# First normalisation of a fused transformer block: from VectorE to ScalarE, with the shift computed on GpSimd

## The chip, the cores and the metric

One core of one Trainium2 chip. The time is device microseconds (us) of one execution. The engines are TensorE (PE in the profile; PEld is its weight load), VectorE (DVE), ScalarE (ACT), GpSimd (POOL) and SyncE (SP, whose queue issues DMAs). The chip's clock for TensorE has two levels, 1.2 and 2.4 GHz; the profile shows the granted share.

## The reference

The input x is 4 x 512 x 512 float32, that is 2048 rows of 512. Four residual blocks follow each other:

```
x = x + fp8_xattn(layernorm(x), ctx)          # stage a
x = x + gated_ffn(layernorm(x), gate, up, down)   # stage b, ternary weights, inner width 1408
x = x + cross_attention(layernorm(x), ctx, mask)  # stage c
x = x + hadamard_quantised_ffn(layernorm(x), ...) # stage d, inner width 2048
```

In stage a the normalised row is cut into blocks of 128, each block is scaled by 448 over its largest absolute value (at least 1e-4), rounded to float8 e4m3, scaled back, and multiplied with the context, which is quantised in blocks of 128 x 128 in the same way. The layernorm is (x - mean) / sqrt(var + 1e-5) per row.

## The kernel before, in words

X holds all rows in on-chip memory as 16 tiles of 128 rows x 512 (line 44). The engines run separate instruction lists, each written out by hand and joined by semaphores; an engine works through its own list strictly in order, so that a wait holds everything behind it. Stages a and b run together in 8 groups (`b_group(g)`, g = 0 to 7), about 33 to 36 us each. Group g does the feed-forward of tiles 2g and 2g+1 (stage b) and, beside it, stage a of tiles n0 = 2g+2 and n1 = 2g+3. Stages c and d follow. Tiles 0 to 2 of stage a are normalised ahead of the groups (lines 1187 to 1207).

Stage b of a group has 11 chunks c. For each, TensorE makes gate and up products (`gate_up_b`, L1725, 16 matmuls, about 1.75 us) in one of two PSUM banks, ScalarE takes Silu of the gate half (`b_silu`, L667), VectorE multiplies it with the up half (`b_hidden`, L1236), ScalarE writes the high half as float16 (`b_high`, L674), GpSimd the remainder (`h_low`, L494), and after all chunks TensorE multiplies down (`b_down`, L1740; the result is scaled and added on VectorE, L1250 and L1252). Chunk n of `gate_up_b` waits until `b_hidden` of chunk n-2 has emptied the bank:

```
wait(pe, b_h_r, n - 1)
```

Stage a of a tile j is spread between these: VectorE takes the row statistics (`a_stats`, L1042 to L1045), GpSimd the root of the variance (`root`, L464), VectorE normalises (`a_normal`, L1050) and takes the block maxima and scales (`a_smalls_of`, L1110, L1114, L1116), ScalarE applies the scales (`a_scale`, L617, L621), VectorE rounds to e4m3 (`a_grids` L1122 and L1124, `a_rounding` L1129 and L1135), SyncE's queue transposes by DMA (`a_turn`, L346), TensorE multiplies (`a_product`, L1677), and VectorE adds the four parts to X (`a_parts`, L1149). Tile n1 is done in the first half of the group, tile n0+2 (which is the next group's n0) is prepared at the end of it.

Around the changed places the lists read:

- GpSimd: `h_low(g, 0)`, `root` of a for n1, `h_low(g, 1)` and on; at the end of the group `root` of b and `b_center` (L470) for n1, `h_low(g, 10)`, `root` of a for n0+2.
- ScalarE: `b_silu` 1 and 2, `b_high` 0, (in group 1 `context_back(1, 3)` L608 and `context_high(1, 3)` L649), `b_silu` 3, in groups 1 to 6 `weight_sums` (L654, three long activations), `b_silu` 4, `b_high` 1 to 3, `a_scale(n1)`. At the end: `b_high` 10, `b_normal(n1)` (L641 and L645, stage b's normalisation with the shift of `b_center` as its bias), in odd groups `context_scaled` (L600), `a_scale(n0 + 2)`, in even groups `context_back` and `context_high`.
- VectorE: `b_hidden` 1, `a_stats(n1)`, `b_hidden` 2, context work, `a_normal(n1)`, context work, `b_hidden` 3 and 4, `a_smalls_of(n1)`, `a_parts(n0, 0)`, `a_grids(n1)`, `b_hidden` 5. At the end: `a_stats(n0 + 2)`, `a_normal(n0 + 2)`, `a_smalls_of(n0 + 2)`, `b_low(n1)` (L1170), in even groups `context_rounding(e, 3)` (L1088, L1090), `b_down(2g)`, `context_low(e, 2)` (L1174); the next group begins with `context_grid` in even groups, `a_grids(n0)`, `b_down` and `b_hidden` 0.

Of the kernel before, what the change touches and what calls it, by code (L numbers as in the profile page):

```python
# [7 lines left out]
P = 128  # L8
# [19 lines left out]
def fused_blocks(nc, x, ctx_t, ctx_n, mask, gate_t, up_t, down_t, gate_s, up_s, down_s,  # L28
# [7 lines left out]
    with ExitStack() as ctx:  # L36
# [16 lines left out]
        shift = sb("shift", [P, 2, 1])  # L53
        room = {"a": "a", "b": "b", "c": "a"}
# [158 lines left out]
        eps_tuple = sem("eps_tuple_ready")  # L213
        c_xh_r, c_xl_r, c_ph_r, c_pl_r, c_cv_hi, c_cv_first, c_cv_lo = (
# [245 lines left out]
        def _(pool):  # L460
            def root(g, j, u):
                r = room[g]
                pool.wait_ge(st_step[g], 3 * j + 3)
                nc.gpsimd.tensor_tensor(rstd[r][:, u, :], mv[r][:, u, 1:2], mhalf[:, :], ALU.pow).then_inc(st_rstd[g], 1)  # L464

# [30 lines left out]
            def b_group(g):  # L496
                more, n0, n1 = g + 1 < PAIRS, 2 * g + 2, 2 * g + 3
                h_low(g, 0)
                if more:
                    root("a", n1, 1)  # L500
                h_low(g, 1)
                h_low(g, 2)
                h_low(g, 3)
                h_low(g, 4)
                h_low(g, 5)
                if more:
                    root("b", n0, 0)
                    b_center(n0, 0)
                h_low(g, 6)
                h_low(g, 7)  # L510
                h_low(g, 8)
                h_low(g, 9)
                if more:
                    root("b", n1, 1)
                    b_center(n1, 1)
                h_low(g, 10)
                if n0 + 2 < NT:
                    root("a", n0 + 2, 0)

# [73 lines left out]
        def _(act):  # L593
# [28 lines left out]

            def a_back(j):
# [56 lines left out]
            def b_group(g):  # L680
# [17 lines left out]
                b_high(g, 0)  # L698
                if g == 1:
                    context_back(1, 3)  # L700
                    context_high(1, 3)
# [60 lines left out]
                if more:  # L762
                    b_normal(n1)
                if odd and following < B:
# [268 lines left out]
        def _(dve):  # L1033
            V = nc.vector

            def stats(g, j, u):
# [3 lines left out]
                if g == "b":  # L1040
                    wait(dve, b_shift, j - 3)
                V.bn_stats(bn[r][:, u, 0:6], tile_of(X, j)).then_inc(s, 1)  # L1042
# [211 lines left out]
            def b_group(g):  # L1254
# [40 lines left out]
                if more:  # L1295
                    a_normal(n1)
# [63 lines left out]
                if n0 + 2 < NT:  # L1360
                    a_normal(n0 + 2)
                    a_smalls_of(n0 + 2)
# [5 lines left out]
                if not odd and e < B and g:  # L1368
                    context_rounding(e, 3)
                if more:  # L1370
# [665 lines left out]
```

## Time and profile before

| | |
|---|---|
| median of 3 runs | 710.25 us (709.42 to 713.08) |
| the profiled execution | 712.37 us, its span 710.5 us |
| busy in the span: PE, DVE, ACT, POOL | 651.9, 573.7, 474.4, 368.0 us |
| groups 1 to 6 of stages a and b | 79.88 to 287.25 us of the span |
| granted clock in these groups | 1.00 of 2.4 GHz |

The busy share is a mean over stages. What a change in the groups is worth has to be read from the chain of waits inside a group: TensorE's list is the longest, and a stall in it is time lost for good. The profile numbers instructions by line of the kernel; where it says `x8` after a row of the timeline, eight like instructions were merged into it.

### The profile page before, as it was taken

The numbers are of one execution on the slowest core, as the hardware profiler recorded it, in microseconds if no ns is written. First come the engines' busy times: TensorE is split into PE (matmuls) and PEld (weight loads), VectorE is DVE, ScalarE is ACT, GpSimd is POOL, SyncE is SP. The second block draws the span as 40 slices with busy tenths as digits, with TensorE's granted clock in tenths as the row PEclk, the third lists the DMA queues.
The fourth block names the chain that finished last, engine by engine and source line by source line (L and its number), as shares of the span: only waits on it lengthen the run. The fifth ranks groups of instructions, "written<-read, shape, count | busy, mean of one in ns | idle before, by whom it ended". The sixth has DMA issues, their size and how long they took to land.

```text
span 710.5 us, 12399 instructions
## 1 busy us (share of the span) xinstructions
PE 651.9 (92%) x4086; PEld 375.4 (53%) x4086; DVE 573.7 (81%) x1255; ACT 474.4 (67%) x981; POOL 368.0 (52%) x291
## 2 busy tenths in 40 slices
PE   1689899999999999998898999897999999999996
PEld 0365566656666676753343444453545555555553
DVE  6889898989898887367687864777888888888874
ACT  3747567856776656378687842576778888778734
POOL 2023122323232413167566730069899999999970
PEclk9999999999999999999999999999999999999998
DMA  9971243434441422718999950344657655656611
GB/s 219 252 259 23 83 102 77 105 90 108 73 111 24 112 67 73 247 30 196 301 285 263 233 98 18 75 86 64 118 120 113 136 108 113 139 118 123 114 47 45
DMA packets 173130, 88.21 MB, mean 124 GB/s; under 512 B 150546, under 2 KB 152594, under 8 KB 172052
## 3 DMA queue, kind: packets, MB, share of 16 engines
q1 hardware_dynamic: 167188, 71.94, 45.5%
q10 hardware_dynamic: 3408, 11.27, 4.8%
q0 software_dynamic: 2480, 4.33, 3.4%
q8 instruction: 28, 0.46, 0.3%
q14 instruction: 26, 0.21, 0.1%
HBM read 51.20 MB, written 4.19 MB: 78 GB/s over the span
## 4 chain that ended last, share of the span: by engine, by line
PE 36%; DVE 28%; ACT 12%; issue 11%; POOL 7%; DMA 4%; SPq 1%; DVEq 0%; POOLq 0%; ACTq 0%
PE ps L1725 10%; PE ps L1820 6%; PE ps L1802 6%; PE ps L1740 4%; DVE y_sm L1549 4%; DMA arena<-arena 3%; PE ps L1878 3%; POOL arena L568 2%; POOL arena L569 2%; DVE ps L1509 2%; DVE arena L1236 2%; PE ps L1950 2%; ACT arena L936 2%; DVE X L1149 2%; ACT arena L919 2%
## 5 line engine op out<-in xcount | busy, mean ns | idle before, releaser
L1725 PE MATMUL ps<-arena 128*128 128x256 f16 x1408 | 161.1, 273 | 6.7 <-DVE arena L1236 4.9
L1725 PEld LDWEIGHTS ps<-arena 128*128 128x128 f16 x1408 | 135.2, 98 | 33.9 <-DVE arena L1236 10.3
L494 POOL TENSOR_TENSOR arena<-arena 128x256 f16<-128x256 f32 x88 | 58.9, 687 | 176.4 <-ACT arena L674 176.3
L1878 PE MATMUL ps<-arena 128*128 128x512 bf16 x512 | 118.9, 380 | 5.6 <-ACT arena L888 3.8
L568 POOL TENSOR_TENSOR arena<-arena 128x1024 f32<-128x1024 f32 x44 | 103.7, 2358 | 31.9 <-DVE arena L1523 28.6
L569 POOL TENSOR_TENSOR arena<-arena 128x1024 f32<-128x1024 f32 x44 | 104.0, 2364 | 0.0
L1740 PE MATMUL ps<-arena 128*128 128x512 f16 x352 | 80.0, 385 | 5.7 <-POOL arena L494 5.7
L1878 PEld LDWEIGHTS ps<-arena 128*128 128x128 bf16 x512 | 48.0, 98 | 65.2 <-DVE arena L1515 7.5
L667 ACT ACTIVATE arena<-ps,gs 128x256 f32<-128x256 f32 x88 | 40.8, 467 | 55.1 <-PE ps L1725 55.1
L1820 PE MATMUL ps<-arena 128*128 128x512 f16 x256 | 59.4, 387 | 6.0 <-DMA arena<-arena 3.5
L1950 PE MATMUL ps<-arena 128*128 128x512 bf16 x256 | 61.4, 386 | 1.9 <-ACT arena L966 1.9
L1740 PEld LDWEIGHTS ps<-arena 128*128 128x128 f16 x352 | 34.2, 99 | 48.5 <-POOL arena L494 9.0
L1509 DVE SCALAR_TENSOR_TENSOR ps<-ps,f_sm,arena 128x512 f32<-128x512 f32 x60 | 45.1, 753 | 17.1 <-ACT arena L910 17.1
L910 ACT ACTIVATE arena<-ps,f_sm 128x512 f32<-128x512 f32 x64 | 44.2, 692 | 17.9 <-PE ps L1878 16.8
L1236 DVE SCALAR_TENSOR_TENSOR arena<-ps,us,arena 128x256 f32<-128x256 f32 x88 | 41.5, 476 | 17.5 <-ACT arena L667 16.6
L1802 PE MATMUL ps<-arena 128*128 128x512 f16 x240 | 53.9, 379 | 1.1 <-DMA arena<-arena 1.1
L936 ACT ACTIVATE arena<-ps 128x512 f16<-128x512 f32 x60 | 35.6, 594 | 26.4 <-DVE ps L1509 26.4
L1515 DVE TENSOR_TENSOR arena<-ps,arena 128x512 f16<-128x512 f32 x60 | 41.3, 688 | 12.7 <-ACT arena L936 12.4
L919 ACT ACTIVATE arena<-arena,y_sm 128x1024 f32<-128x1024 f32 x32 | 36.3, 1144 | 17.7 <-DVE y_sm L1561 17.7
L1820 PEld LDWEIGHTS ps<-arena 128*128 128x128 f16 x256 | 25.2, 100 | 37.8 <-DMA arena<-arena 4.5
L1149 DVE SCALAR_TENSOR_TENSOR X<-ps,a_sm,X 128x512 f32<-128x512 f32 x56 | 41.8, 747 | 2.6 <-PE ps L1677 1.4
L674 ACT ACTIVATE arena<-arena 128x256 f16<-128x256 f32 x88 | 33.4, 408 | 10.6 <-DVE arena L1236 10.4
(168 smaller groups left out, 1187.3 us busy)
## 6 DMA issues: line engine op xcount, KB each, us to landing
arena<-in_ctx_t SPq DMA_DIRECT2D x7, 1024.0 KB, 6.0
arena<-in_wg_t SPq DMA_DIRECT2D x16, 256.0 KB, 3.7
arena<-in_wu_t SPq DMA_DIRECT2D x16, 256.0 KB, 4.3
arena<-in_wd_t SPq DMA_DIRECT2D x16, 256.0 KB, 5.2
arena<-in_ctx_n SPq DMA_DIRECT2D x4, 1024.0 KB, 11.4
arena<-in_wu_t ACTq DMA_DIRECT2D x4, 1024.0 KB, 6.0
arena<-in_wd_t ACTq DMA_DIRECT2D x4, 1024.0 KB, 5.9
out_x<-X SPq DMA_DIRECT2D x16, 256.0 KB, 2.5
```

Source lines behind the costliest of these rows:

```text
L494: nc.gpsimd.tensor_tensor(hl[:, c, at:at + 2 * P], b_h[n % 4], hh[:, c, at:at + 2 * P], ALU.subtract).then_inc(b_hl_r, 1)
L568: nc.gpsimd.tensor_tensor(b[:, :, 0, :], a[:, :, 0, :], a[:, :, 1, :], ALU.add).then_inc(d_bfp, 1)
L569: nc.gpsimd.tensor_tensor(b[:, :, 1, :], a[:, :, 0, :], a[:, :, 1, :], ALU.subtract).then_inc(d_bfp, 1)
L1149: V.scalar_tensor_tensor(tile_of(X, j), bank(2 + b), a_sm[:, u, 3, b:b + 1], tile_of(X, j), ALU.mult, ALU.add).then_inc(a_add if b == KD - ...
L1236: V.scalar_tensor_tensor(b_h[n % 4], bank(n % 2)[:, 2 * P:4 * P], us[:, c:c + 1], b_sil[n % 2], ALU.mult, ALU.mult).then_inc(b_h_r, 1)
L1509: V.scalar_tensor_tensor(h_last[:, D * n:D * n + D] if at(k, NT - 1) else up, up, f_sm[:, u, 5:6], d_sil[n % 2], ALU.mult, ALU.mult).then_ ...
L1725: last = M(bank(n % 2)[:, 2 * P * i:2 * P * i + 2 * P], W[:, b, c * P:c * P + P], part[:, b, at:at + 2 * P], start=(b == 0 and part is xhT ...
L1740: last = M(bank(6 + j % 2), part[:, c, at:at + P], dW[:, c, :], start=(c == 0 and part is hh), stop=(c == C0 - 1 and part is hl))
L1802: last = M(bank(2 + u), rows[slot(k)][:, b, :], part[:, 0, b, :], start=(b == 0 and rows is c_xhT and part is high), stop=(b == KD - 1 and ...
L1820: last = M(bank(6 + u), rows[slot(j)][:, b, :], part[:, 1, b, :], start=(b == 0 and rows is c_phT and part is high), stop=(b == KD - 1 and ...
L1878: last = M(bank(2 * (n % 2) + i), d_qT[u][:, b, :], W[:, b, D * n:D * n + D], start=(b == 0), stop=(b == KD - 1))
L1950: last = M(bank(down_bank(j)), yqT[u][:, c, :], Wd[:, c, :], start=(c == 0), stop=(c == C1 - 1))
```

## The change

For tiles 3 to 15 of stage a the normalisation leaves VectorE. GpSimd computes the shift, minus mean times rstd, right behind the root (`a_center`), and ScalarE applies both in one activation that writes the same buffer (`a_normal` in its list: behind `b_high` 0 for n1, behind `b_normal(n1)` for n0+2). VectorE's `a_smalls_of(n0 + 2)` moves behind `b_low(n1)` and, in even groups, behind `context_rounding(e, 3)`; `a_smalls_of(n1)` stays where it was. `a_center` comes in 13 times; the waits that guard the small buffers are added to `root` and `stats`.

```diff
--- before.py
+++ after.py
@@ -51,6 +51,7 @@
             bn[r], mv[r], carrier[r] = sb("bn_" + r, [P, 2, 9]), sb("mv_" + r, [P, 2, 2]), sb("carrier_" + r, [P, 2])
             rstd[r] = sb("rstd_" + r, [P, 2, 1])
         shift = sb("shift", [P, 2, 1])
+        shift_a = sb("shift_a", [P, 2, 1])
         room = {"a": "a", "b": "b", "c": "a"}
         mv_d = sb("mv_d", [P, NT, 2])
         rstd_d, shift_d = sb("rstd_d", [P, NT, 1]), sb("shift_d", [P, NT, 1])
@@ -211,6 +212,7 @@
         c_shift, d_shift = sem("c_shift"), sem("d_shift")
         d_stat, d_root = sem("d_stat"), sem("d_root")
         eps_tuple = sem("eps_tuple_ready")
+        a_shift = sem("a_shift")
         c_xh_r, c_xl_r, c_ph_r, c_pl_r, c_cv_hi, c_cv_first, c_cv_lo = (
             sem("c_" + n) for n in ("x_high", "x_low", "p_high", "p_low", "ctx_high", "ctx_first_low", "ctx_low"))
         c_xq, c_pq = ([sem(f"{n}_turned{u}") for u in range(3)] for n in ("c_x", "c_p"))
@@ -461,7 +463,14 @@
             def root(g, j, u):
                 r = room[g]
                 pool.wait_ge(st_step[g], 3 * j + 3)
+                if g == "a":
+                    wait(pool, a_xn_r, j - 1)
                 nc.gpsimd.tensor_tensor(rstd[r][:, u, :], mv[r][:, u, 1:2], mhalf[:, :], ALU.pow).then_inc(st_rstd[g], 1)
+
+            def a_center(j, u):
+
+                pool.wait_ge(st_rstd["a"], j + 1)
+                nc.gpsimd.tensor_scalar(shift_a[:, u, :], mv["a"][:, u, 0:1], -1.0, rstd["a"][:, u, :], ALU.mult, ALU.mult).then_inc(a_shift, 1)
 
             def b_center(j, u):
 
@@ -498,6 +507,7 @@
                 h_low(g, 0)
                 if more:
                     root("a", n1, 1)
+                    a_center(n1, 1)
                 h_low(g, 1)
                 h_low(g, 2)
                 h_low(g, 3)
@@ -516,6 +526,7 @@
                 h_low(g, 10)
                 if n0 + 2 < NT:
                     root("a", n0 + 2, 0)
+                    a_center(n0 + 2, 0)
 
             for g in range(PAIRS):
                 b_group(g)
@@ -620,6 +631,12 @@
                 wait(act, a_add, j - 1)
                 nc.scalar.activation(a_sm[:, u, 3, :], a_sm[:, u, 1, :], ACT.Copy, scale=ctop[:, j // 4, 0:1]).then_inc(a_back_r, 1)
 
+            def a_normal(j):
+                u = j % 2
+                act.wait_ge(a_shift, j - 2)
+                nc.scalar.activation(a_xn[u], tile_of(X, j), ACT.Identity, bias=shift_a[:, u, :],
+                                     scale=rstd["a"][:, u, :]).then_inc(a_xn_r, 1)
+
             def a_back(j):
                 u = j % 2
                 act.wait_ge(a_round, 4 * j + 4)
@@ -696,6 +713,8 @@
                 b_silu(g, 1)
                 b_silu(g, 2)
                 b_high(g, 0)
+                if more:
+                    a_normal(n1)
                 if g == 1:
                     context_back(1, 3)
                     context_high(1, 3)
@@ -761,6 +780,8 @@
                     context_high(1, 1)
                 if more:
                     b_normal(n1)
+                if n0 + 2 < NT:
+                    a_normal(n0 + 2)
                 if odd and following < B:
                     context_scaled(following, 1)
                     context_scaled(following, 2)
@@ -1039,6 +1060,8 @@
                 wait(dve, st_rstd[g], j - 1)
                 if g == "b":
                     wait(dve, b_shift, j - 3)
+                if g == "a":
+                    wait(dve, a_shift, j - 4)
                 V.bn_stats(bn[r][:, u, 0:6], tile_of(X, j)).then_inc(s, 1)
                 dve.wait_ge(s, 3 * j + 1)
                 V.memset(carrier[r][:, u:u + 1], 0.0).then_inc(s, 1)
@@ -1292,8 +1315,6 @@
                 if g == 0:
                     context_low(0, 2)
                     context_low(0, 3)
-                if more:
-                    a_normal(n1)
                 if not odd and e < B and g:
                     context_rounding(e, 1)
                 if g == 0:
@@ -1357,9 +1378,6 @@
                     dve.wait_ge(ds_r, 1)
                 if not odd and e < B and g:
                     context_low(e, 1)
-                if n0 + 2 < NT:
-                    a_normal(n0 + 2)
-                    a_smalls_of(n0 + 2)
                 if more:
                     b_low(n1)
                 if g == 0:
@@ -1367,6 +1385,8 @@
                     context_low(1, 1)
                 if not odd and e < B and g:
                     context_rounding(e, 3)
+                if n0 + 2 < NT:
+                    a_smalls_of(n0 + 2)
                 if more:
                     b_down(2 * g)
                 if not odd and e < B and g:
```

## Rows read from the trace of the kernel before

**Rows 1.** Windows: group 4; busy us per engine, then clock, DMA share, GB/s

```profile
185.00:220.53 35.53, 33.20 (x238) 22.49 (x237) 33.02 (x68) 24.72 (x71) 10.81 (x17) 1.00 0.34 89
```

**Rows 2.** Waits of TensorE, 42 to 290 us: total, times, longest

```profile
PE ps L1740 <- POOL arena L494: 5.7, 5, 1.9
PE ps L1725 <- DVE arena L1236: 4.9, 9, 1.2
```

**Rows 3.** Groups of instructions, 60 to 310 us: the normalisation on VectorE

```profile
L1050 DVE TENSOR_SCALAR arena<-X,mv_a,rstd_a 128x512 f32<-128x512 f32 x12 | 6.5, 544 | 8.7 <-POOL rstd_a L464 8.4
```

**Rows 4.** Timeline of group 4: start, duration, instruction, idle before

```profile
191.96 0.67 POOL L494 TENSOR_TENSOR arena<-arena 128x256 f16<-128x256 f32 x1 [12.01 <-ACT arena L674]
192.59 0.82 POOL L464 TENSOR_TENSOR rstd_a<-mv_a,mhalf 128x1 f32<-128x1 f32 x1
...
192.85 0.47 ACT L667 ACTIVATE arena<-ps,gs 128x256 f32<-128x256 f32 x1 [0.97 <-PE ps L1725]
195.06 0.46 ACT L667 ACTIVATE arena<-ps,gs 128x256 f32<-128x256 f32 x1
195.42 1.02 ACT L674 ACTIVATE arena<-arena 128x256 f16<-128x256 f32 x3
...
195.31 0.87 DVE L1236 SCALAR_TENSOR_TENSOR arena<-ps,us,arena 128x256 f32<-128x256 f32 x2
...
200.12 3.87 PE L1725 MATMUL ps<-arena 128*128 128x256 f16 x32 [0.34 <-DVE arena L1236]
```

**Rows 5.** Timeline: the shift of stage b and its activation

```profile
102.28 0.27 POOL L470 TENSOR_SCALAR shift<-mv_b,rstd_b 128x1 f32<-128x1 f32 x1 [0.17 <-POOL rstd_b L464]
...
102.59 0.81 ACT L641 ACTIVATE arena<-X,shift,rstd_b 128x512 f32<-128x512 f32 x1 [1.62 <-POOL shift L470]
...
144.42 0.77 POOL L470 TENSOR_SCALAR shift<-mv_b,rstd_b 128x1 f32<-128x1 f32 x1 [0.17 <-POOL rstd_b L464]
```

**Rows 6.** Timeline of group 5, around chunk 4

```profile
227.49 1.00 POOL L464 TENSOR_TENSOR rstd_a<-mv_a,mhalf 128x1 f32<-128x1 f32 x1
...
229.96 0.46 ACT L667 ACTIVATE arena<-ps,gs 128x256 f32<-128x256 f32 x1
...
230.46 0.48 DVE L1236 SCALAR_TENSOR_TENSOR arena<-ps,us,arena 128x256 f32<-128x256 f32 x1 [0.92 <-ACT arena L667]
```

**Rows 7.** Timeline of group 3, around chunk 4

```profile
158.20 0.55 POOL L464 TENSOR_TENSOR rstd_a<-mv_a,mhalf 128x1 f32<-128x1 f32 x1
...
160.87 0.87 DVE L1236 SCALAR_TENSOR_TENSOR arena<-ps,us,arena 128x256 f32<-128x256 f32 x2
```

**Rows 8.** Timeline of group 1, around chunk 4

```profile
88.16 0.55 POOL L464 TENSOR_TENSOR rstd_a<-mv_a,mhalf 128x1 f32<-128x1 f32 x1
...
87.34 1.26 ACT L608 ACTIVATE arena<-arena,crel 128x128 f32<-128x128 f32 x4
...
89.18 0.46 ACT L667 ACTIVATE arena<-ps,gs 128x256 f32<-128x256 f32 x1
...
91.86 0.48 DVE L1236 SCALAR_TENSOR_TENSOR arena<-ps,us,arena 128x256 f32<-128x256 f32 x1
```

**Rows 9.** Timeline from group 2 into group 3

```profile
146.07 0.63 ACT L645 ACTIVATE arena<-arena 128x512 f16<-128x512 f32 x1
148.16 1.28 ACT L617 ACTIVATE arena<-arena,a_sm 128x128 f32<-128x128 f32 x4 [1.45 <-DVE a_sm L1116]
...
150.82 0.63 ACT L649 ACTIVATE arena<-arena 128x512 f16<-128x512 f32 x1
...
147.02 0.69 DVE L1110 TENSOR_REDUCE a_sm<-arena 128x4 f32<-128x512 f32 x1
...
149.94 0.68 DVE L1250 TENSOR_TENSOR arena<-ps,ds_bc 128x512 f32<-128x512 f32 x1
...
154.22 0.48 DVE L1236 SCALAR_TENSOR_TENSOR arena<-ps,us,arena 128x256 f32<-128x256 f32 x1
```

**Rows 10.** Timeline at the end of group 0

```profile
76.06 0.69 DVE L1170 TENSOR_TENSOR arena<-arena 128x512 f16<-128x512 f32 x1 [1.14 <-ACT arena L645]
```

## The prediction

> **What bounds the kernel now.** I read the page for the whole, the windows of the groups for the stage that the change touches, TensorE's waits for what a gain there could be, and the timeline of all four engines for the order inside a group. The window of group 4 shows two engines about equally full: TensorE 33.20 us and VectorE 33.02 us of 35.53 us, ScalarE only 24.72 us [rows 1]. TensorE's list decides the time, as its matmuls follow each other nearly without gaps; VectorE decides how large the gaps are. In the stretch of the groups TensorE waited 4.9 us, in 9 places, for `b_hidden` (L1236), and 5.7 us for GpSimd's remainder (L494) [rows 2]. The first is what a lighter VectorE could give back.
>
> One of these places comes in every group from 1 to 6: chunk 7 of `gate_up_b` waits for `b_hidden` 5. In group 4 it starts at 200.12 us after 0.34 us of idling [rows 4]. Between `b_hidden` 4 and 5 VectorE has the scales of n1, half of `a_parts` and the grids, without a pause: from the start of `b_hidden` 4 to TensorE's chunk 7 it is 4.4 us (195.31 us plus half of 0.87 us, to 200.12 us [rows 4]). So whatever delays `b_hidden` 4 delays TensorE by as much. This is the place that decides the change.
>
> **What is removed.** The normalisation on VectorE takes 0.544 us, 12 times in this window and once ahead of it, and VectorE waited 8.4 us for GpSimd's root before 7 of them [rows 3]. 13 x 0.544 us = 7.1 us of work and up to 8.4 us of waiting go. This helps TensorE only through the 4.9 us above.
>
> **What is added in the first half of a group.** The activation on ScalarE stands between `b_high` 0 and `b_silu` 3. It needs the shift, the shift needs the root, and the root stands behind `h_low` 0 on GpSimd, which in turn waits for the `b_high` 0 just issued: ScalarE waits for a chain that begins at its own last instruction. Behind the waiting activation are queued `b_silu` 3, `weight_sums` and `b_silu` 4. I price it from the start of the root. The root takes 0.55 us at its shortest [rows 7]; the shift begins 0.17 us later, takes 0.27 us, and the activation starts 0.04 us after that [rows 5]: 1.03 us. The activation takes 0.81 us [rows 5], but ScalarE's next instruction starts 0.10 us before the end of the one ahead of it (195.06 us for 0.46 us, next at 195.42 us [rows 4]), so 0.71 us. From `b_silu` 3 to `b_silu` 4 it is 195.06 - 192.85 = 2.21 us [rows 4], weight sums included. And a VectorE that stands ready starts `b_hidden` 4 0.50 us behind `b_silu` 4 (229.96 to 230.46 us, with 0.92 us of waiting [rows 6]). Sum: `b_hidden` 4 starts 4.45 us behind the start of the root, plus what the root exceeds 0.55 us.
>
> - Group 4: 192.59 + 4.45 + 0.27 = 197.31 us against 195.31 + 0.39 = 195.70 us [rows 4], so +1.6 us. Group 2 has the same pattern in the trace, +1.6 us.
> - Group 3: 158.20 + 4.45 = 162.65 us against 160.87 + 0.40 = 161.27 us [rows 7], so +1.4 us.
> - Group 5: 227.49 + 4.45 + 0.45 = 232.39 us against 230.46 us [rows 6], so +1.9 us.
> - Group 1: the activation also stands ahead of `context_back` and `context_high`, which take 89.18 - 87.34 = 1.84 us and were done while GpSimd worked [rows 8]. 88.16 + 4.45 + 1.84 = 94.45 us against 91.86 us [rows 8], so +2.6 us.
> - Group 0 has no weight sums and group 6 a VectorE held by the mask rows. I take 1.2 us each, an estimate a little under the least that I counted, 1.4 us.
>
> Together 1.6 + 1.6 + 1.4 + 1.9 + 2.6 + 2.4 = 11.5 us. The two instructions that VectorE no longer has there don't help: it then stands before `b_hidden` 3 and 4 earlier and waits for ScalarE. The DMA transpose of n1 and its product come later by the same amount as the matmuls around them; GpSimd's shift takes 0.27 us of an engine that idled 12.01 us before `h_low` 0 [rows 4], and costs nothing but what stands in the chain.
>
> **What moves at a group's end.** From even to odd, ScalarE's float16 copy ends at 146.07 + 0.63 = 146.70 us, and VectorE then does `b_low`, `context_rounding` and only now the maxima. These three took 149.94 - 147.02 = 2.92 us in the old order [rows 9]. With 0.1 us for the two handoffs, `a_scale` starts at 149.8 us, not at 148.16 us: +1.6 us. `context_back` and `context_high` stand behind it on ScalarE (the latter at 150.82 us [rows 9]), VectorE's `context_low(e, 2)` waits for them, and behind that stand `a_grids`, `b_down` and `b_hidden` 0 at 154.22 us [rows 9], for which chunk 2 of TensorE waits with no slack that I can see. Two such passages, 2 -> 3 and 4 -> 5: 3.2 us. From group 0 to 1 the maxima stood in a time in which VectorE waited 1.14 us more for `b_low` [rows 10]; moved behind it they are added to the chain, +1.0 us (the 2.92 us of rows 9 less `b_low` and two roundings of about 0.65 us each leave the maximum and its two small followers). From odd to even the new activation, 0.71 us, comes in ahead of `context_scaled` and `a_scale`; I take 0.4 us twice, an estimate of about half of it, between 0 and all of it. From 5 to 6 VectorE idles and nothing is lost. Together 5.0 us.
>
> **Sum.** 11.5 + 5.0 = 16.5 us. The profiled execution would go from 712.37 to 728.9 us; it stood 2.1 us above the median of the runs, 710.25 us, so that the median becomes 726.8 us. Stages c and d are not touched and only start later.
>
> **Costs that the trace does not show.** The new shift may meet VectorE. The same instruction took 0.27 us at one place and 0.77 us at another [rows 5]; nothing can make it shorter than 0.27 us. I took 0.27 us, as it is the usual one; with 0.77 us in all 7 groups it is 3.5 us more, 730.3 us. The cost of the passages lies between 0 (VectorE's relief covers them) and the 5.0 us counted. The Trainium skill (SBUF — State Buffer, section "SBUF: two separate sides") says that VectorE and GpSimd take one shared pair of ports as an exclusive lock, so that the later one stands still for the whole instruction of the other. By that rule the added shift would often be the 0.77 us kind, and the sum would be nearer 730 us than 727 us; the 0.77 us row agrees, the 0.27 us row shows that it is not always so.
>
> **Rivals.**
>
> *Faster: VectorE was the bound, and relief wins.* The place is `gate_up_b`'s wait for `b_hidden`. If ScalarE's chain were not late at `b_hidden` 4, at most the 4.9 us of rows 2 come back: 710.25 - 4.9 = 705.4 us. For it speaks VectorE's 33.02 of 35.53 us; against it that in group 5 VectorE already waited 0.92 us for ScalarE at `b_hidden` 4 [rows 6], so that ScalarE's chain is the one behind. It decides from the point where the activation starts 1.4 us or more earlier than I count, for instance if GpSimd had the root done before `h_low` 0; the list does not allow it. The Trainium skill (Perfetto Trace Analysis, section "Identifying the Most-Contended Engine") says to work on the engine with the highest occupancy first, and by occupancy VectorE's relief should pay. Chance 0.09.
>
> *Only the first half costs.* The relief of VectorE at the group's end, with waits for the root of 8.4 us over 7 places [rows 3], covers the passages: 710.25 + 11.5 = 721.8 us, and less, down to 714 us, if a part of the first term is also covered. Chance 0.17.
>
> *No change.* Gains and losses cancel, or the delays are made good in waits of TensorE that are already there, such as the 5.7 us for L494: 707 to 714 us. Against it: those waits hang on the same VectorE and ScalarE lists and move along. Chance 0.05.
>
> *Dearer than 732 us,* by more blocking between GpSimd and VectorE or by a delay that passes twice. Chance 0.05.
>
> My forecast, 722 to 732 us, has 0.64. A measurement of this kernel can tell about 0.5%, 3.6 us, from no change. Slower by more than that: 0.64 + 0.17 + 0.05 = 0.86; same 0.05; faster 0.09. The range from 714 to 732 us leaves out 0.19.
>
> **What would show it.** In the changed profile ScalarE waits, 6 or 7 times and about 2 us each (from 191.96 us, where `h_low` 0 starts, to 193.9 us [rows 4]), for GpSimd's new shift before the new activation; `b_hidden` (L1236 of before) at chunk 4 waits for Silu 1.5 to 2 us in groups 2 to 5; TensorE's waits for `b_hidden` grow from 4.9 us to some 18 us; VectorE's waits for rstd_a are gone, and its busy time is 7 us less. Group 4 lasts about 37.5 us in place of 35.53 us. If VectorE's wait at chunk 4 is short and TensorE's waits shrink, I am wrong at the first half; if the groups grow by only 1.6 us and the group starts show no new wait, at the passages.

## The result, and the profile after

The changed kernel is slower, and by more than I had forecast: 734.74 us median of 4 runs (732.13 to 738.2), against 711.66 us (709.42 to 714.28) for the kernel before beside it, ratio 1.033 (1.0287 to 1.0373). I had said 726.8 us and a range up to 732.0 us; the median lies 2.7 us above it. Medians here are over all executions of a kernel; the ratios leave out the few that were slow as a whole, which comes with any kernel. The profiled execution took 734.13 us, its span is 732.2 us.

I read the changed profile in the order of the prediction. First the busy times of the page:

```profile
PE 655.0 (89%) x4055; PEld 379.0 (52%) x4086; DVE 569.4 (78%) x1242; ACT 484.0 (66%) x994; POOL 372.0 (51%) x304
```

VectorE did 573.7 us before and does 569.4 us now; ScalarE has risen from 474.4 to 484.0 us. The work moved as the change says, and the kernel is 21.7 us of span longer. That can't be seen in busy times. It is seen in the windows of groups 1 to 6 (the columns are those of [rows 1]):

```profile
83.17:122.53 39.36, 35.13 (x240) 23.78 (x241) 33.23 (x69) 27.20 (x77) 10.21 (x19) 0.96 0.34 88
122.53:162.00 39.47, 34.70 (x238) 23.48 (x236) 33.18 (x67) 25.48 (x70) 11.77 (x19) 0.96 0.36 82
162.00:198.99 36.99, 33.29 (x241) 23.05 (x240) 30.11 (x65) 26.48 (x75) 10.21 (x19) 1.00 0.35 92
198.99:240.30 41.31, 36.32 (x237) 23.81 (x237) 33.19 (x67) 26.91 (x75) 11.68 (x19) 0.92 0.29 77
240.30:276.66 36.36, 34.25 (x237) 23.65 (x236) 26.76 (x55) 22.71 (x61) 10.65 (x19) 0.95 0.27 66
276.66:311.14 34.48, 32.69 (x238) 22.94 (x236) 25.04 (x46) 19.50 (x53) 9.43 (x17) 1.00 0.30 71
```

Two things are to be seen. Every group is longer: group 4 takes 41.31 us for the 35.53 us of [rows 1]. And the third column from the right, the granted clock, is no longer 1.00 everywhere: 0.96, 0.96, 0.92, 0.95 in groups 1, 2, 4 and 5. In group 4 TensorE's busy time rose by 3.1 us (33.20 to 36.32 us) for the same matmuls. I had no term for that.

The waits of 42 to 310 us say who waits for whom (total, times, longest; L1745 is the L1725 of before, L1259 `b_hidden`, L637 the new activation, L473 the new shift):

```profile
DVE arena L1259 <- ACT arena L684: 18.5, 17, 2.0
...
PE ps L1745 <- DVE arena L1259: 15.6, 11, 2.1
...
DVE arena L1193 <- ACT arena L662: 14.9, 7, 3.4
...
ACT arena L637 <- POOL shift_a L473: 13.7, 7, 2.3
```

ScalarE waits for the shift in 7 places, 2.0 us on average. VectorE, which was to be relieved, waits 18.5 us for Silu (before: 3.2 us) and 14.9 us for the float16 copy ahead of `b_low` (before: 4.0 us). TensorE's waits for `b_hidden` went from 4.9 us [rows 2] to 15.6 us. Here is one such place, chunk 4 of group 4, to be laid beside [rows 4] (timeline: start, duration, instruction, idle before):

```profile
206.29 0.67 POOL L503 TENSOR_TENSOR arena<-arena 128x256 f16<-128x256 f32 x1 [11.99 <-ACT arena L691]
206.91 0.82 POOL L468 TENSOR_TENSOR rstd_a<-mv_a,mhalf 128x1 f32<-128x1 f32 x1
207.83 0.59 POOL L473 TENSOR_SCALAR shift_a<-mv_a,rstd_a 128x1 f32<-128x1 f32 x1
208.46 0.81 ACT L637 ACTIVATE arena<-X,shift_a,rstd_a 128x512 f32<-128x512 f32 x1 [2.26 <-POOL shift_a L473]
209.19 0.46 ACT L684 ACTIVATE arena<-ps,gs 128x256 f32<-128x256 f32 x1
...
211.38 0.46 ACT L684 ACTIVATE arena<-ps,gs 128x256 f32<-128x256 f32 x1
...
211.87 0.48 DVE L1259 SCALAR_TENSOR_TENSOR arena<-ps,us,arena 128x256 f32<-128x256 f32 x1 [1.71 <-ACT arena L684]
...
216.44 5.29 PE L1745 MATMUL ps<-arena 128*128 128x256 f16 x32 [2.11 <-DVE arena L1259]
```

From the start of the root to `b_hidden` 4 it is 4.96 us; my step gave 4.45 + 0.27 = 4.72 us, and the shift took 0.59 us here where I took 0.27 us. VectorE stands 1.71 us before `b_hidden` 4, and 4.57 us later TensorE starts chunk 7 after 2.11 us of idling, where it idled 0.34 us before. So far this is the forecast. But the 32 matmuls then take 5.29 us; in [rows 4] they took 3.87 us. The window of what follows that stall:

```profile
216.44:220.00 3.56, 3.56 (x18) 2.56 (x19) 3.13 (x5) 1.99 (x7) 1.30 (x2) 0.53 0.19 37
```

TensorE was granted 0.53 of its clock on average over these 3.56 us, which is nearly all at 1.2 GHz in place of 2.4 GHz. In the 3.90 us ahead of the stall it had 1.00.

Over all groups: from chunk 2 of group 0 (44.14 us after, 43.55 us before) to the start of group 7 (311.28 and 287.39 us) the changed kernel needs 23.3 us more; the rest of the span is 2.2 us shorter (420.9 us for 423.1 us).

### The profile page after: what moved, and what is told of

Its sections match the earlier page's. It is cut to its first block, busy times and chain, and to the rows that moved or that the text cites. A ratio compares the mean times of both kernels' runs of the same rounds, so it can differ in the third digit from the quotient of the medians.

```text
span 732.2 us, 12394 instructions
## 1 busy us (share of the span) xinstructions
PE 655.0 (89%) x4055; PEld 379.0 (52%) x4086; DVE 569.4 (78%) x1242; ACT 484.0 (66%) x994; POOL 372.0 (51%) x304
## 4 chain that ended last, share of the span: by engine, by line
PE 29%; DVE 22%; issue 21%; ACT 13%; POOL 10%; DMA 3%; SPq 1%; POOLq 0%; DVEq 0%; ACTq 0%
PE ps L1745 8%; PE ps L1840 6%; PE ps L1822 6%; DVE y_sm L1569 4%; POOL arena L579 2%; DMA arena<-arena 2%; POOL arena L503 2%; POOL arena L580 2%; PE ps L1898 2%; DVE ps L1529 2%; ACT arena L957 2%; PE ps L1697 2%; ACT arena L940 2%; DVE X L1172 2%; ACT arena L671 2%
## 5 line engine op out<-in xcount | busy, mean ns | idle before, releaser
L1745 PE MATMUL ps<-arena 128*128 128x256 f16 x1408 | 167.7, 279 | 18.9 <-DVE arena L1259 15.6
L1745 PEld LDWEIGHTS ps<-arena 128*128 128x128 f16 x1408 | 139.0, 100 | 48.7 <-DVE arena L1259 20.4
L1898 PE MATMUL ps<-arena 128*128 128x512 bf16 x486 | 115.6, 380 | 7.2 <-ACT arena L909 4.0
L1259 DVE SCALAR_TENSOR_TENSOR arena<-ps,us,arena 128x256 f32<-128x256 f32 x88 | 41.9, 477 | 33.8 <-ACT arena L684 32.9
L1970 PE MATMUL ps<-arena 128*128 128x512 bf16 x251 | 59.1, 379 | 2.0 <-ACT arena L987 1.8
L1760 PEld LDWEIGHTS ps<-arena 128*128 128x128 f16 x352 | 34.3, 99 | 49.2 <-POOL arena L503 9.8
L1535 DVE TENSOR_TENSOR arena<-ps,arena 128x512 f16<-128x512 f32 x60 | 41.3, 688 | 12.7 <-ACT arena L957 12.4
L1840 PEld LDWEIGHTS ps<-arena 128*128 128x128 f16 x256 | 25.2, 99 | 37.7 <-DMA arena<-arena 4.2
```

Source lines behind the costliest of these rows:

```text
L1745: last = M(bank(n % 2)[:, 2 * P * i:2 * P * i + 2 * P], W[:, b, c * P:c * P + P], part[:, b, at:at + 2 * P], start=(b == 0 and part is xhT ...
L1760: last = M(bank(6 + j % 2), part[:, c, at:at + P], dW[:, c, :], start=(c == 0 and part is hh), stop=(c == C0 - 1 and part is hl))
L1840: last = M(bank(6 + u), rows[slot(j)][:, b, :], part[:, 1, b, :], start=(b == 0 and rows is c_phT and part is high), stop=(b == KD - 1 and ...
L1898: last = M(bank(2 * (n % 2) + i), d_qT[u][:, b, :], W[:, b, D * n:D * n + D], start=(b == 0), stop=(b == KD - 1))
L1970: last = M(bank(down_bank(j)), yqT[u][:, c, :], Wd[:, c, :], start=(c == 0), stop=(c == C1 - 1))
```

## The experiments

I made eleven runs. Two of them repeat a kernel unchanged, to see what is chance. My theory is that of the forecast, that lists waiting for each other stall TensorE, with one addition: the half clock behind those stalls makes up the part I hadn't counted. The rivals are that ScalarE is simply given too much work, that the part not counted lies elsewhere, and that it is chance. The quoted expectations give them letters and say how each run should come out.

**One half of the change at a time.** `first_half` keeps the activation of n1 and puts the group's end back:

```diff
-                    a_center(n0 + 2, 0)
...
-                if n0 + 2 < NT:
-                    a_normal(n0 + 2)
...
+                if n0 + 2 < NT:
+                    a_normal(n0 + 2)
+                    a_smalls_of(n0 + 2)
                 if more:
                     b_low(n1)
...
-                if n0 + 2 < NT:
-                    a_smalls_of(n0 + 2)
```

> Only the tiles n1 (3, 5, ... 15) are normalised on ScalarE; tiles 4, 6, ... 14 and their block maxima are done on VectorE as before. Theory A (two separate costs, each made larger by TensorE's clock): the waits of TensorE at chunk 7 stay at 1.4 to 2.1 us in groups 1 to 6, three of them (groups 2, 4, 5) are followed by about 3.5 us at half clock, 1.6 us lost each; time before + 11.5 + 4.8 = + 16 us. Rival B (the group's end costs nothing, all is lost in the first half): the whole + 23 us. Rival C (the group's end is the dear part): + 8 us or less.

`group_end` does the reverse: `a_center(n1, 1)` and ScalarE's `a_normal(n1)` are gone and VectorE normalises n1 again, at its old place.

> Only the tiles n0+2 (4, 6, ... 14) are normalised on ScalarE, with the block maxima behind b_low; tiles 3, 5, ... 15 stay on VectorE. Theory A: TensorE's new waits are 1.6 us at chunk 2 of groups 3 and 5, 0.4 us more in 2 and 4, 1 us in group 1; none is long enough for the clock to drop behind it, so + 5 us. Rival B: 0. Rival C: + 15 us.

Measured: `first_half` 731.67 us, ratio 1.0264 (1.022 to 1.0309); `group_end` 717.33 us, ratio 1.0097 (1.0062 to 1.0132); the kernel before beside them 710.74 us. To the start of group 7 `first_half` loses 13.3 us and `group_end` 6.2 us in their traces, where my terms were 11.5 and 5.0 us. In `group_end` TensorE's waits ahead of chunk 2 tell the passages apart, here those into groups 1, 3 and 4:

```profile
86.74 7.08 PE L1744 MATMUL ps<-arena 128*128 128x256 f16 x48 [2.24 <-DVE arena L1256]
...
159.91 5.42 PE L1744 MATMUL ps<-arena 128*128 128x256 f16 x48 [1.70 <-DVE arena L1256]
...
194.71 5.41 PE L1744 MATMUL ps<-arena 128*128 128x256 f16 x48 [0.87 <-DVE arena L1256]
```

Into groups 1 to 5 they are 2.24, 0.86, 1.70, 0.87 and 1.70 us; before, 1.18, 0.49, 0, 0.48 and 0 us. The sum has grown by 5.2 us, and my terms were 1.0, 0.4, 1.6, 0.4 and 1.6 us. Behind the first stall the 48 matmuls take 7.08 us and not 5.42 us: 1.7 us of half clock, of which a later wait takes up 0.5 us (TensorE waits 0.54 us for L1174 there in the kernel before, and not at all here). That is 6.4 us for the 6.2 us of the trace.

One part of the expectation for `first_half` missed: half clock behind three of the stalls at chunk 7. The stalls came as expected, 2.11 to 2.12 us in groups 2, 4 and 5, and behind none of them did the clock fall. Here is the one in group 4:

```profile
211.50 3.87 PE L1743 MATMUL ps<-arena 128*128 128x256 f16 x32 [2.11 <-DVE arena L1256]
```

The half clock cost time in group 0 alone, where the product of stage a took 3.42 us, in the kernel before 1.90 us. 13.3 - 1.5 = 11.8 us is what the first half costs without it, for my 11.5 us.

The median of `first_half` is the odd one: 21 us above the kernel before, with 13.3 us of them in the groups. In its trace 5.9 us more lie behind the groups (429.0 us for 423.1 us), in code that neither change touches. Stage c has a stall there that none of my terms is about (timeline of TensorE):

```profile
363.80 5.03 PE L1838 MATMUL ps<-arena 128*128 128x512 f16 x16 [5.08 <-DMA arena<-arena]
```

**TensorE kept busy through the stalls.** `fill` adds useless matmuls into an unused bank: ahead of chunk 7 in groups 1 to 6, at the start of group 1, and ahead of the last chunk of the first down product in groups 0, 2 and 4. All else stays:

```diff
+                if c == 7 and 1 <= g < PAIRS - 1:
+                    fill_wait(7, 6)
...
+                    if j in (0, 4, 8) and c == C0 - 1:
+                        fill_wait(7, 5)
...
+                if g == 1:
+                    fill_wait(0, 8)
```

> The changed kernel with matmuls of no use (float32 128 x 128 into a free bank, 0.24 us each) placed in TensorE's list ahead of the long waits: 6 before chunk 7 in groups 1 to 6, 8 at the start of group 1, 5 before the last chunk of the down product in groups 0, 2 and 4. Theory A (the excess over the forecast is TensorE's clock after stalls of about 2 us): the granted clock stays at 1.00 in the groups, the waits for VectorE stay as long when the filling is counted in, and the time falls by about 5 x 1.6 = 8 us to some 726 us. Rival D (the clock has no part, the stalls alone are the excess): the same time as the change or some us more.

Measured: 734.31 us (732.13 to 736.08), ratio 1.0319 (1.0272 to 1.0366). In the trace the fillers do what a cost of the clock lets one expect: group 2 takes 37.83 us for 39.47 us and group 4 takes 37.71 us for 41.31 us, 5.2 us together. Group 0, which has no filler at its longest stall (2.51 us, ahead of the products of stage a), loses 4.2 us there and 2.7 us in the changed kernel (from chunk 2 to group 1), so that up to group 7 it is 20.1 us for 23.3 us. Behind the groups `fill` takes 2.2 us longer than the changed kernel (423.1 us for 420.9 us), and the median, for which I had expected some 726 us, is within 1 us of that of the changed kernel. So I ran the changed kernel once more without an edit (`changed_again`) and, beside it, all fillers with one more in group 0 (`fill_all`: `fill_wait(5, 10)` ahead of `max_spread(1)`).

> The changed kernel once more, in five rounds on one chip with the next. Its groups 1 to 6 depend on nothing that varies, so they start within 1 us of where they did, and the half clock comes at the same stalls (behind the waits of about 2 us in groups 0, 2, 4 and 5). Stages c and d vary by several us from one execution to another. Time: + 22 to + 25 us against the kernel before.

> The run fill, with 10 more useless matmuls in group 0, ahead of the wait for the block maxima of the context. Theory A (stalls of about 2 us cost a second time through the clock, 5 us in groups 2 and 4 and 1.6 us or more in group 0): granted clock 1.00 throughout the groups, group 7 starts at about 305 us of the span in place of 311 us, and the median is 4 to 6 us under that of the changed kernel of the same call. Rival D: the groups may end earlier but the median stays, because stages c and d take the time back.

Measured: `changed_again` 737.21 us (733.44 to 742.24), ratio 1.0368 (1.0316 to 1.0419); `fill_all` 731.89 us (726.76 to 739.11), ratio 1.0256 (1.0204 to 1.0307); before 711.82 us. The repetition was worth most. The same code, the same chunk 7 of group 4, behind the same wait (timeline of `changed_again`):

```profile
214.63 3.87 PE L1745 MATMUL ps<-arena 128*128 128x256 f16 x32 [2.11 <-DVE arena L1259]
```

And the windows of the stretch behind it and of the group:

```profile
216.50:220.00 3.50, 3.47 (x25) 2.28 (x25) 3.39 (x10) 3.33 (x10) 1.19 (x2) 1.00 0.54 108
...
197.21:234.88 37.67, 33.20 (x237) 22.47 (x237) 32.63 (x67) 25.19 (x70) 11.68 (x19) 1.00 0.32 84
```

The stall is 2.11 us again, but the clock stays at 1.00, the 32 matmuls take 3.87 us, and the group 37.67 us. The half clock behind such a stall comes in one execution and stays away in another. My expectation, the same half clock at the same stalls, missed: it was there again in groups 0, 1 and 5 and stayed away in groups 2 and 4, so that group 7 starts 3.8 us sooner behind chunk 2 of group 0 than in the first profile. With the filler in its place the group takes 37.71 us (`fill_all`, timeline of TensorE and window of group 4):

```profile
214.34 1.50 PE L1728 MATMUL ps<-I 128*128 128x128 f32 x12
...
216.61 3.87 PE L1747 MATMUL ps<-arena 128*128 128x256 f16 x32 [0.77 <-DVE arena L1259]
```

```profile
199.14:236.85 37.71, 35.65 (x259) 25.14 (x258) 32.68 (x67) 25.25 (x70) 11.65 (x19) 1.00 0.32 84
```

So 37.7 us is the length of group 4 at full clock, the stall itself included. And in group 0 the product of stage a (L1697) took 3.59 us in the changed kernel, behind 2.51 us of idling (its timeline):

```profile
52.17 0.39 PE L1711 MATMUL ps<-cmx_diag,ones 16*128 16x16 f32 x2 [2.51 <-DVE cmx_diag L1088]
52.49 3.59 PE L1697 MATMUL ps<-arena 128*128 128x512 f16 x8
```

With the filler it takes 1.90 us, and group 0 loses 1.2 us in place of 2.7 us, both from chunk 2 to group 1. Up to group 7 `fill_all` loses 18.2 us in all. It isn't at full clock throughout, as I had expected: in group 1 a stall without filler, which the half clock at the group's start had shortened in the changed kernel, now stands in full, and the clock falls behind it (`fill` takes 5.41 us there, behind a stall of 2.24 us):

```profile
89.34 7.04 PE L1747 MATMUL ps<-arena 128*128 128x256 f16 x48 [2.23 <-DVE arena L1259]
```

The medians of `fill_all` and `changed_again` lie 5.3 us apart, which agrees with the half clock in size. The intervals of their ratios just miss each other (1.0307 and 1.0316), but single executions overlap, and `fill` showed no such gain; so in the median the gain is likely and not shown.

**The chain of waits without the work.** If the lists' mutual waiting is the cause, the activation must cost nothing where nobody waits for it. `root_first` makes the chain shorter by one step on GpSimd:

```diff
-                h_low(g, 0)
                 if more:
                     root("a", n1, 1)
                     a_center(n1, 1)
+                h_low(g, 0)
```

> The changed kernel with one order changed on GpSimd: root and shift of n1 ahead of h_low 0, so that they no longer start behind ScalarE's b_high 0. Theory A (ScalarE waits for a chain that begins at its own last instruction): the activation of n1 starts about 1.1 us earlier in groups 1 to 6, TensorE's waits at chunk 7 fall to about 0.3 to 1 us, the half clock behind them is gone; 7 + 5 us less than the change, about 722 us. Rival E (the activation's own 0.8 us on ScalarE is what costs, not the wait for GpSimd): within 2 us of the change.

Measured: 723.41 us, ratio 1.0173 (1.0111 to 1.0235); to group 7 it loses 12.4 us, for 20.1 us in `fill` beside it. No half clock follows its stalls at chunk 7, but these are still 0.43 to 1.79 us long, not the 0.3 to 1 us that I expected. ScalarE still waits, but less (waits of ScalarE in the groups; 13.7 us in 7 places in the changed kernel):

```profile
ACT arena L637 <- POOL shift_a L473: 7.8, 7, 1.7
```

A part of what is left is the shift itself, which in this order meets VectorE: in groups 0, 2 and 4 it takes 0.97 us (timeline of group 4):

```profile
202.54 0.97 POOL L473 TENSOR_SCALAR shift_a<-mv_a,rstd_a 128x1 f32<-128x1 f32 x1
...
202.78 0.68 DVE L1111 TENSOR_TENSOR arena<-arena 128x512 f32<-128x512 f32 x1
```

`late` leaves GpSimd's list alone and moves ScalarE's activation behind `b_silu` 4, by which time the shift is long there:

```diff
-                if more:
-                    a_normal(n1)
...
                 b_silu(g, 4)
+                if more:
+                    a_normal(n1)
```

> The changed kernel with the activation of n1 behind b_silu 4, not ahead of b_silu 3. By then GpSimd has the shift ready, ScalarE waits for nothing, and Silu 3, the weight sums and Silu 4 start as in the kernel before. Theory A: the first half costs under 1 us in all (the block maxima start 0.2 to 0.3 us later in groups 1, 2, 4 and 5), what is left is the group's end; 717 us, like the run group_end. Rival E (ScalarE's 0.8 us per tile is the cost): 722 us or more.

Measured: 718.42 us (714.93 to 722.97), ratio 1.0098 (1.0065 to 1.0131). In the timeline of group 4:

```profile
198.92 0.46 ACT L684 ACTIVATE arena<-ps,gs 128x256 f32<-128x256 f32 x1
...
199.28 0.81 ACT L637 ACTIVATE arena<-X,shift_a,rstd_a 128x512 f32<-128x512 f32 x1
...
200.12 0.69 DVE L1133 TENSOR_REDUCE a_sm<-arena 128x4 f32<-128x512 f32 x1 [0.22 <-ACT arena L637]
...
204.07 3.87 PE L1745 MATMUL ps<-arena 128*128 128x256 f16 x32 [0.43 <-DVE arena L1259]
```

The activation follows Silu at once, with no wait; VectorE's maxima wait 0.22 us for it; TensorE waits 0.43 us at chunk 7 instead of 2.11 us. What is left, 4.6 us to group 7, I put down to the group's end: TensorE's waits ahead of chunk 2 of groups 1 to 5 have grown by 5.1 us, as in `group_end`.

`late_maxback` is `late` with `a_smalls_of(n0 + 2)` put back ahead of `b_low(n1)`; `late_n1` has the activation of n1 alone, at the late place, and the group's end of before.

> The run late, with the block maxima of n0+2 back ahead of b_low. In the even groups a_scale then starts 0.3 us later than in the kernel before and not 1.6 us later, in group 0 the maxima fall into the wait for b_low again. Theory A: 712 to 714 us, within the noise of the kernel before; with all 13 activations still on ScalarE. Rival E: 718 us or more. Nothing here makes it clearly faster than before, as the 4.9 us of waits that a lighter VectorE could give back do not hang on VectorE alone.

> The kernel before with one edit: tiles n1 are normalised on ScalarE, behind b_silu 4; everything at the group's end is as before. Theory A: both causes are gone though 7 of the 13 activations remain, so 711 to 713 us, the same as the kernel before, the block maxima of n1 0.2 to 0.3 us late. Rival E (the activation's time on ScalarE costs): 716 us or more.

Measured: `late_maxback` 715.17 us, ratio 1.0051 (1.0025 to 1.0078), 3.3 us under `late` and a little over the 712 to 714 us that I expected. (One of its ten executions took 3471.58 us; it is not in the ratio, and I don't know its cause.) TensorE's waits ahead of chunk 2 of groups 1 to 5 are 2.23, 0.84, 1.68, 0.79 and 1.68 us in `late`, and 1.76, 0.63, 0, 0.66 and 0 us here: the order of the maxima costs 1.7 us in each of the passages 2 -> 3 and 4 -> 5, as I had counted, but only 0.5 us in 0 -> 1, where I had put 1.0 us. Up to group 7 the two traces differ by 0.7 us alone (4.6 and 3.9 us), less than these waits. The trace shows where most of the rest went: in `late_maxback` TensorE idles ahead of chunk 0, 1.82 us at group 1 (0.85 us in `late`) and 0.26, 0.56, 0.23, 0.58 and 0.23 us at groups 2 to 6, where `late` shows no wait. At group 1:

```profile
79.78 1.19 SPq L356 DMA_TRANSPOSE arena<-arena  x1
...
82.29 3.65 PE L1745 MATMUL ps<-arena 128*128 128x256 f16 x32 [1.82 <-issue]
```

The transpose of the low half can't start before `b_low`, which now stands behind the maxima, and TensorE starts 2.51 us after it, at group 2 as well (116.70 and 119.21 us). So neither order of the maxima is free.

`late_n1` 712.12 us over 12 runs, beside 710.92 us over 23, ratio 1.0013 (0.9984 to 1.0041), and in the trace it needs 0.3 us less than the kernel before up to group 7. Seven activations of 0.81 us on ScalarE, and the time is that of before. Too much work for ScalarE is not the cause in the first half: the work costs nothing measurable there, while `first_half`, with the same work behind a wait, lost 13.3 us in its trace. The waits of TensorE in 42 to 290 us agree with [rows 2] (5.8 us for 4.9 us, 5.7 us for 5.7 us):

```profile
PE ps L1743 <- DVE arena L1256: 5.8, 11, 1.2
...
PE ps L1758 <- POOL arena L503: 5.7, 5, 1.9
```

**The half clock in the kernel before.** It has one such place too: 24 matmuls of `b_down` at 72.19 us take 6.96 us, behind a wait of 1.92 us for GpSimd; the granted clock is 0.57 from 72.10 to 76.00 us and 1.00 after that. `before_fill` keeps TensorE busy there, in the kernel before:

```diff
+                    if j in (0,) and c == C0 - 1:
+                        fill_wait(7, 7)
```

> The kernel before with 7 useless matmuls ahead of the last chunk of the first down product of group 0, where its trace has a wait of 1.92 us and half clock behind it. Theory A: the clock in that stretch stays at 1.00 and the down product's last 24 matmuls take 5.35 us, not 6.96 us; group 1 starts at most 0.9 us earlier, as it then waits for the transposes of tile 3. The median moves by less than can be told. Rival D (the half clock there has another cause than the wait): the clock falls there as before.

Measured: 714.42 us (709.17 to 717.39), ratio 1.0023 (0.9991 to 1.0054). Its trace, TensorE into group 1:

```profile
70.28 1.72 PE L1708 MATMUL ps<-I 128*128 128x128 f32 x14
...
72.37 5.35 PE L1742 MATMUL ps<-arena 128*128 128x512 f16 x24 [0.36 <-POOL arena L494]
...
80.04 3.65 PE L1725 MATMUL ps<-arena 128*128 128x256 f16 x32 [2.32 <-issue]
```

The same in the kernel before:

```profile
72.19 6.96 PE L1740 MATMUL ps<-arena 128*128 128x512 f16 x24 [1.92 <-POOL arena L494]
...
79.88 3.65 PE L1725 MATMUL ps<-arena 128*128 128x256 f16 x32 [0.73 <-issue]
```

The matmuls are 1.61 us quicker, and TensorE then idles 1.59 us longer (2.32 us for 0.73 us) ahead of group 1, which starts at 80.04 us, not earlier than 79.88 us. A half clock costs nothing where a wait behind it takes it up. Group 1 of the changed kernel shows the same: its first 32 matmuls take 5.32 us, in `fill` 3.65 us, the wait ahead of chunk 2 is 0.56 us for 2.24 us, and the group has 39.36 us for 39.38 us. What I wrote ahead of the prediction, that a stall in TensorE's list is time lost for good, is too strong.

**Is the time of `first_half` chance?** The same kernel again:

> The run first_half once more, to see what of its time comes back in a second profile: its groups took 13.3 us more than those of the kernel before, its time 21 us more, and the rest lay in stage c, where TensorE waited 5.08 and 2.10 us for DMA transposes and ran at half clock behind them. If stage c's waits are fixed by the groups' new timing (theory F), they are there again, of 5 us and 2 us, and the part behind the groups is 428 to 430 us. If they are chance (theory G), other waits stand there and the part behind the groups is some other number between 420 and 430 us; the time stays between 728 and 733 us.

Measured: 727.1 us (723.69 to 735.2), ratio 1.0165 (1.0076 to 1.0254), the kernel before beside it at 715.8 us (708.95 to 719.09). Its profiled execution, 735.2 us, was by far the longest of its four, so I take no lengths from it, and theories F and G stay undecided. The median fell under the 728 to 733 us that I had expected under either; the two runs of this kernel stand 21 and 11 us above the kernel before beside them, so up to 10 us of the distance do not come back.

## Why the prediction was wrong in size

The sign and the mechanism were right; the sum was short. By its steps:

**First half of a group, 11.5 us: right.** `fill` shows groups 1 to 6 at full clock, `fill_all` all but group 1. Against before, groups 1 to 6 of `fill` grew by 3.6, 2.3, 3.2, 2.2, 3.7 and 1.0 us; my terms, both halves together, were 3.6, 2.0, 3.0, 2.0, 3.5 and 1.2 us. Group 0 was to be 1.2 us and is 1.2 us with its filler. `first_half` alone gives 11.8 us. That the sum fits so closely is in part luck: groups 2 to 5 cost 0.2 to 0.3 us more than I counted and group 6 0.2 us less, and the 1.2 us of groups 0 and 6 were estimates. ScalarE's wait for the shift was to be about 2 us in 6 or 7 places; it is 13.7 us in 7. TensorE's waits for `b_hidden` were to be some 18 us and are 15.6 us. Group 4 was to last about 37.5 us; it takes 37.7 us at full clock. `late` and `late_n1` take the wait away and keep the work, and the loss of the first half is gone.

**Group's end, 5.0 us: right.** 5.2 us of waits in `group_end`, passage by passage as counted; only which part of it the passage 0 -> 1 owes to the maxima was too much. "Only the first half costs" falls.

**Stalls priced once: this step failed.** The prediction held that "from the start of `b_hidden` 4 to TensorE's chunk 7 it is 4.4 us" and "whatever delays `b_hidden` 4 delays TensorE by as much". The delay was right; that TensorE then goes on at its old speed was an assumption that I didn't state. The sum had no term for the clock, although the trace of before shows the thing itself at 72.19 us. In the changed kernel's profiled execution it cost 1.5 us in group 0, 1.6 us in group 2 and 3.6 us, in two places, in group 4, read as the length less that of the same group with fillers: 6.7 us. The clock fell in groups 1 and 5 too, but these are no longer than with fillers. In group 1 the wait ahead of chunk 2 took it up, as said above. In group 5 the half clock behind chunk 7 costs 1.5 us, but the wait of 1.68 us that `fill` has ahead of chunk 2 is gone, as group 4 ended late (36.36 us for 36.64 us). 23.3 - 6.7 = 16.6 us are left for the terms that came to 16.5 us. The three other traces of this kernel, with and without fillers, give nearly the same once the half clock in them is taken off: 16.7 us in `changed_again` (19.5 less 1.5 in group 0 and 1.4 in group 5), 16.6 us in `fill_all` (18.2 less 1.6 in group 1), 17.1 us in `fill` (20.1 less 2.9 in group 0). The rest of the span is 2.2 us shorter, which leaves 21.7 us of span.

What the median owes to the clock can't be told so exactly. `changed_again` had none of it in group 4, lost 19.5 us up to group 7, and its median was 25.4 us above the kernel before beside it. So a part of the distance is behind the groups, and there a second sentence of the prediction doesn't hold, that stages c and d "are not touched and only start later": from group 7 to the end the profiled executions of the variants take between 420 and 429 us, the changed kernel 420.9 and 426.4 us in its two. In the second, TensorE waits 4.03 and 1.98 us for transposes in stage c and does the 16 matmuls behind each in 5.31 us, in the first in 3.63 us. Of the 5.2 us that `fill` saved in groups 2 and 4, its group 0 lost 1.5 us again and the part behind the groups 2.2 us; why the median shows nothing at all, I can't settle. How much of the 8 us between 726.8 and 734.74 us is owed to the clock and how much to stages c and d stays open.

**The shift's slow kind: came at two places of 13.** L473 took 0.264 us at the median and 0.595 us at most, in groups 2 and 4, so VectorE and GpSimd holding each other up added 0.33 us twice and not 3.5 us. At both places VectorE was in L1111, which reads two operands from on-chip memory, and the shift ended 0.12 us after it (207.83 + 0.59 = 208.42 us in group 4):

```profile
207.62 0.68 DVE L1111 TENSOR_TENSOR arena<-arena 128x512 f32<-128x512 f32 x1
```

The 0.97 us shifts of `root_first` ended 0.04 to 0.06 us after a VectorE instruction of the same kind, and the 0.77 us shift of [rows 5] 0.05 us after one (L1174), while a shift under a reduction (L1082, 2.28 us) took 0.27 us. The rule of the Trainium skill (SBUF — State Buffer, section "SBUF: two separate sides") has a condition that the prediction left out: the lock is for VectorE instructions in a two-port mode or with two inputs in SBUF. With it the rule agrees with these rows, and the two shifts that met such an instruction add 0.7 us, not 3.5 us. That the time came out above 730 us is no support for the prediction's use of it.

**VectorE's relief: as said, of no use.** Its waits for rstd_a are gone. Its busy time fell by 4.3 us, not by 7: the normalisation fell from 8.7 to 1.6 us, and the other 2.8 us are spread over other rows, none over 0.7 us. What it gained turned into waits of 18.5 and 14.9 us. The Trainium skill's advice to start at the engine with the highest occupancy (Perfetto Trace Analysis, section "Identifying the Most-Contended Engine") doesn't help in this stage: at 33.02 of 35.53 us VectorE was almost the fullest engine, and taking 7 normalisations off it (`late_n1`) or all 13 (`late_maxback`), with no wait in the first half, made the kernel no faster than before (712.12 us for 710.92 us, 715.17 us for 711.82 us). The 3.3% of the change itself come from the waits.

**The rival on the other side** needed the root ahead of `h_low` 0. `root_first` did that, and lost 12.4 us up to group 7 all the same. Even `late_n1`, without the wait, only draws level: the 4.9 us of [rows 2] didn't come back.

## What to carry to other kernels

Before an instruction is moved to an emptier engine, look at what it waits for there and what is queued behind it: here the activation waited for a chain that began with the instruction just ahead of it, and two Silus later it cost nothing that could be measured. A price for a stall of TensorE has a second part, the clock behind it, which belongs in the upper end of the range and not in the middle, since it doesn't come each time. When a filler or a repair shows in the trace but not in the median, repeat the unedited kernel before believing either.

## What the runs showed of the hardware that I hadn't expected

**The clock behind a short stall.** In the groups of the changed kernel TensorE's granted clock was 0.52 to 0.68 on average over the 3.5 to 3.6 us behind six stalls of 1.5 to 2.5 us, and 32 matmuls took 5.29 us for 3.87 us. The same stall of 2.11 us at the same chunk was followed by 0.53 in one execution and by 1.00 in another, in `first_half` three such stalls by full clock. The length of the stall alone doesn't decide it: in one trace, that of the changed kernel, 24 matmuls behind 1.48 us take 7.03 us in group 4 and 5.35 us in group 2, and behind 1.93 us in group 0 also 5.35 us. What does decide it no run here shows. Where useless matmuls filled most of the stall, groups 2 and 4 had 37.7 to 37.8 us each in two kernels.

**DMA transposes of stage c.** TensorE's wait for them, in code that no variant touches, differs widely. In the profiled executions the longest in each was 1.80 us in the kernel before, 1.66 us in the changed one, 4.03 us in its repetition, and 5.08 us in `first_half`. In `group_end` it was this:

```profile
364.14 5.24 PE L1839 MATMUL ps<-arena 128*128 128x512 f16 x16 [12.19 <-DMA arena<-arena]
```

That one wait is twice what `group_end` changes in the groups, and what sets it stays open. It is the reason why I compared the groups up to the start of group 7 and not the spans.
